# Graph layer 1: projecting the nodes and fetching values by index instead of projecting per edge

## The reference, cut to what matters

```
x = _layernorm(x + L0(x, adj))
Xq = x @ W_lin.T;  Xv = x @ W_val.T              # (32, 256, 128), 4 heads of 32
Qs = Xq[:, src];  Kt = Xq[:, dst]                # 256 edges
e  = einsum(leaky_relu(Qs + Kt, 0.2), a) + log(adj[src, dst] + 1e-8)
attn = softmax of e over the edges of one src
Y  = segment_sum(attn * Xv[:, dst], src)
x  = _layernorm(x + Y @ W_out.T)
```

## Time and profile before

| | us |
|---|---|
| median of 3 runs | 551.41 (551.0 to 552.96) |
| the profiled execution | 550.63 |
| its span, first to last instruction | 548.9 |
| busy: DVE / ACT / POOL | 415.2 / 371.9 / 203.4 |

### The profile page before, as it was taken

One profiled execution on the slowest core, in us unless ns is written; L12 is line 12 of the kernel. 1 busy time (PEld: TensorE's weight loads), 2 busy tenths in 40 slices (PEclk: granted clock), 3 DMA queues, 4 the chain that ended last, 5 costly groups with the idle time before them and its releaser, 6 DMA issues.

```text
span 548.9 us, 11011 instructions
## 1 busy us (share of the span) xinstructions
PE 526.6 (96%) x3516; PEld 463.3 (84%) x3516; DVE 415.2 (76%) x1465; ACT 371.9 (68%) x752; POOL 203.4 (37%) x245
## 2 busy tenths in 40 slices
PE   7999998999999899999999999999999999999964
PEld 6998535688888889989989989989999998989953
DVE  5899677998686463588696786787687776679796
ACT  4776794777656544366787686795785787686773
POOL 4970352257674305027136037027126016110213
PEclk9999999999999999999999999999999999999987
DMA  6631000222100000000001000000100100100002
GB/s 191 188 95 41 0 0 20 72 75 66 39 0 1 2 1 1 1 1 1 1 2 41 0 1 17 21 0 0 38 0 0 38 1 1 38 2 1 21 19 77
DMA packets 28419, 15.29 MB, mean 28 GB/s; under 512 B 2353, under 2 KB 28081, under 8 KB 28385
## 3 DMA queue, kind: packets, MB, share of 16 engines
q1 hardware_dynamic: 27536, 13.38, 8.5%
q0 software_dynamic: 560, 1.25, 0.8%
q10 hardware_dynamic: 288, 0.26, 0.2%
HBM read 10.69 MB, written 4.19 MB: 27 GB/s over the span
## 4 chain that ended last, share of the span: by engine, by line
PE 83%; DVE 11%; POOL 2%; ACT 2%; issue 1%; POOLq 0%; DVEq 0%
PE psum L293 15%; PE psum L295 15%; PE psum L294 15%; PE psum L2135 10%; PE psum L1934 5%; PE psum L1982 3%; PE psum L2077 3%; PE psum L2087 3%; PE psum L1993 2%; PE psum L2181 2%; PE psum L1997 2%; PE psum L2163 2%; PE psum L2006 2%; DVE soft L1087 1%; PE psum L2155 1%
## 5 line engine op out<-in xcount | busy, mean ns | idle before, releaser
L209 POOL TENSOR_TENSOR ln_r<-ln_v,mhalf 128x8 f32<-128x8 f32 x25 | 41.7, 1666 | 203.6 <-DVE ln_v L203 203.6
L2135 PE MATMUL psum<-l2w_s,h 128*128 128x128 f32 x512 | 59.7, 275 | 0.0
L2135 PEld LDWEIGHTS psum<-l2w_s,h 128*128 128x128 f32 x512 | 59.0, 192 | 0.6
L293 PE MATMUL psum<-qt_hi,l2w_s_hi 128*128 128x512 f32 x128 | 52.8, 413 | 0.0
L295 PE MATMUL psum<-qt_hi,l2w_s_lo 128*128 128x512 f32 x128 | 50.7, 396 | 0.0
L294 PE MATMUL psum<-qt_lo,l2w_s_hi 128*128 128x512 f32 x128 | 50.6, 395 | 0.0
L287 ACT ACTIVATE keep_x<-keep_x,ln_b,ln_r (+1 forms) x104 | 42.7, 486 | 2.6 <-POOL ln_b L212 2.6
L1664 ACT ACTIVATE h<-psum 128x512 f32<-128x512 f32 x60 | 34.8, 594 | 11.7 <-PE psum L295 11.6
L293 PE MATMUL psum<-wgt_hi,h_hi 128*128 128x256 f32 x128 | 37.1, 290 | 0.9 <-DVE h_lo L1064 0.9
L295 PE MATMUL psum<-wgt_hi,h_lo 128*128 128x256 f32 x128 | 35.8, 279 | 0.0
L294 PE MATMUL psum<-wgt_lo,h_hi 128*128 128x256 f32 x128 | 35.7, 279 | 0.0
(11 more groups left out here) (297 smaller groups left out, 1748.7 us busy)
## 6 DMA issues: line engine op xcount, KB each, us to landing
keep_x<-in_x SPq DMA_DIRECT2D x32, 128.0 KB, 3.0
xin<-in_x SPq DMA_DIRECT2D x32, 128.0 KB, 2.2
out_x<-ob SPq DMA_DIRECT2D x24, 128.0 KB, 1.8
out_x<-keep_x SPq DMA_DIRECT2D x8, 128.0 KB, 2.0
l2w_raw<-in_l2w POOLq DMA_DIRECT2D x1, 512.0 KB, 4.8
adjs<-in_adj_t ACTq DMA_DIRECT2D x2, 128.0 KB, 2.7
adjs<-in_adj SPq DMA_DIRECT2D x2, 128.0 KB, 3.0
l2w_s<-in_l2w POOLq DMA_DIRECT2D x1, 256.0 KB, 4.8
```

Source lines behind the costliest of these rows:

```text
L209: pool.tensor_tensor(ln.r[:].rearrange("p s k -> p (s k)"), ln.v[:].rearrange("p s k -> p (s k)"), mhalf[:], ALU.pow).then_inc(ln.root, 1)
L293: pe.matmul(o, lhs[0], rhs[0], start=start, stop=False)
L2135: i = pe.matmul(bank(s)[:, 0, k * D:(k + 1) * D], h2[:, s, g, j * N + t * P:j * N + (t + 1) * P], l2w3_s[:, g, :], start=(g == 0), stop=(g ...
```

## The change

xn is transposed on PE (`turn_x1`), copied by ACT to x1t, and both projections run over the 256 nodes of a slot: queries (`project(q, 0)`) and values (`project(q, 1)`). The queries are split by ACT and DVE (`q_high`, `q_low`) into qn, and `select` multiplies them with a selection matrix of 256 columns. The values are copied by ACT to vst, stored by SP to internal memory, and fetched by POOL into vall with indirect DMAs, one row per edge's destination, in four chunks of four slots (`collect_v`). The split of xn goes; POOL gets bn_out of the pairs 4 to 7 from ACT; ACT scales two of the four tiles of slot 0 that DVE scaled. The matmuls that bring the sorted edge ends into columns (L1920) are made for the destinations too. The orders of all engines are new and the loops are written out. The core of the diff, in the order SP, POOL, DVE, ACT, PE:

```diff
-            lambda c: (sb("sel", [P, T, 2, E], F32R, c),
+            lambda c: (sb("sel", [P, T, E], F32R, c), sb("log_a", [P, E], scope=c), sb("esb", [P, 2, ET, P // 2], scope=c),
...
+        v_rows = [nc.dram_tensor(f"v_rows{c}", (N, CB * D), F32, kind="Internal").ap() for c in range(CHUNKS)]
+        v_nat = [v.rearrange("(t n) (b d) -> n t b d", n=P, b=CB) for v in v_rows]
...
+            def load_pair(p):
                 for s in range(2):
                     sp.wait_ge(ln0.added, 2 * p + s - 1)
                     load_x(s, 2 * p + s)
+            def store_v(p):
+                for s in range(2):
+                    q = 2 * p + s
+                    sp.wait_ge(v_out, q + 1)
+                    for t in range(T):
+                        sp.dma_start(v_nat[q // CHUNKS][:, t, 2 * (q % CHUNKS):2 * (q % CHUNKS) + 2, :],
+                                     vst[:, s, t, :, :]).then_inc(v_stored[s], 16)
+            for p in range(1, 3):
+                load_pair(p)
+            for p in range(IT):
+                if p + 3 < IT:
+                    load_pair(p + 3)
+                store_v(p)
...
+            link(pool.tensor_copy(dst_rows[:], sorted_col[:, 1, :]))
...
-            def split_x1(p, s, first):
...
+            def bn_out(p):
+                for s in range(2):
+                    q = 2 * p + s
+                    pool.wait_ge(bnt_ready, q)
+                    pool.wait_ge(t1_done, q - 1)
+                    pool.tensor_scalar(bnt[:, s, :], oraw[:, q, :], bco[:, 2, 2:3], bco[:, 3, 2:3], ALU.mult,
+                                       ALU.add).then_inc(bnt_ready, 1)
+            def collect_v(c):
+                for s in range(2):
+                    pool.wait_ge(v_stored[s], 32 * 2 * (c + 1))
+                for t in range(ET):
+                    pool.indirect_dma_start(vall[:, t, c * CB:(c + 1) * CB, :].rearrange("p b d -> p (b d)"), None,
+                                            v_rows[c],
+                                            bass.IndirectOffsetOnAxis(ap=dst_rows[:, t:t + 1], axis=0)).then_inc(v_here, 16)
+            for p in range(1, IT - 2):
+                if p + 3 < IT:
+                    bn_out(p + 3)
+                for s in range(2):
+                    pool.wait_ge(ln0_done[s], 2 * (p + 2))
+                ln_power(pool, p + 2, ln0)
+                if p in (2, 4):
+                    collect_v(p // 2 - 1)
...
+            collect_v(2)
             for s in range(2):
                 first_power(pool, s, ln1, True)
+            collect_v(3)
...
+            def stats0(p):
+                wait_apart(dve, dc, ln0.added, 2 * p + 2)
+                for s in range(2):
+                    for k in range(4):
+                        i = dve.bn_stats(ln0.st[:, s, k, :], row(p)(s, k // 2, k % 2))
+                i.then_inc(ln0.stats, 2)
+            def moments0(p):
+                dve.wait_ge(ln0.stats, 2 * p)
+                for s in range(2):
+                    for k in range(4):
+                        i = dve.bn_aggr(ln0.ag[:, s, k, :], ln0.st[:, s, k, :])
+                i.then_inc(ln0.mean, 1)
+                if p == 3:
+                    dve.wait_ge(ln0.one_root, 6)
+                else:
+                    dve.wait_ge(ln0.rstd, p - 3)
                 ln_var_eps(dve, p, ln0)
             def apply0(p):
                 dve.wait_ge(ln0.rstd, p + 1 - ln0.late)
-                for k in range(4):
+                for k in (0, 2):
                     y = row(p)(0, k // 2, k % 2)
                     i = dve.tensor_scalar(y, y, ln0.ag[:, 0, k, 0:1], ln0.r[:, 0, k:k + 1], ALU.subtract, ALU.mult)
-                i.then_inc(ln0_done[0], 2)
+                i.then_inc(ln0_done[0], 1)
+            def q_low(q):
+                dve.wait_ge(q_hi, q + 1)
+                dve.tensor_tensor(qn[1][:, q % 2], projected_bank(q % 2, 0), qn[0][:, q % 2], ALU.subtract).then_inc(q_lo, 1)
...
             first_moments(dve, 3, ln0, False)
-            x1_low(2)
-            leaky_slot(0, 0)
+            q_low(0)
+            sum0_slot(2, 0)
             first_apply(dve, 3, ln0, range(4), ln0_done[1], 2)
-            sum0_slot(2, 0)
             first_stats(dve, 4, ln0)
-            x1_low(3)
             first_moments(dve, 4, ln0, False)
             sum0_slot(2, 1)
-            leaky_slot(0, 1)
+            q_low(1)
             first_stats(dve, 5, ln0)
             first_apply(dve, 4, ln0, range(4), ln0_done[0], 2)
             first_moments(dve, 5, ln0, False)
+            leaky_slot(0, 0)
             sum0_slot(3, 0)
             first_apply(dve, 5, ln0, range(4), ln0_done[1], 2)
+            leaky_slot(0, 1)
             sum0_slot(3, 1)
...
+            stats0(3)
+            q_low(2)
+            moments0(3)
+            q_low(3)
+            for p in range(2, IT - 2):
+                leaky(p - 1)
+                if p == IT - 3:
+                    take_scores(0)
+                sum0(p + 2)
+                apply0(p + 1)
+                stats0(p + 2)
+                q_low(2 * p)
+                moments0(p + 2)
+                q_low(2 * p + 1)
             maxima(0)
+            leaky(IT - 3)
             apply0(IT - 1)
-            leaky(IT - 3)
             normalize(0)
+            q_low(2 * (IT - 2))
             take_attention(0)
+            q_low(2 * (IT - 2) + 1)
+            leaky(IT - 2)
...
-                leaky_slot(IT - 2, s)
                 weighted_low(0, s)
+            q_low(Q - 2)
             def xs_low(q):
                 dve.wait_ge(xs_hi, q + 1)
                 dve.tensor_tensor(xs[1][:, q], xn[:, q], xs[0][:, q], ALU.subtract).then_inc(xs_lo, 1)
-            weighted_low(1, 0)
             add(0, 0, o1_done, 1, ln1)
             first_stats(dve, 0, ln1)
             first_moments(dve, 0, ln1, True)
+            q_low(Q - 1)
+            weighted_low(1, 0)
             weighted_low(1, 1)
             add(0, 1, o1_done, 6, ln1)
...
+            x1_turned(0)
             bn_out_slot(2, 1, False)
             first_scale(act, 1, ln0, (1, 3), ln0_done[1])
...
             projected(0, 0)
-            x1_high_both(3)
+            x1_turned(1)
+            for s in range(2):
+                bn_out_slot(3, s, False)
             projected(0, 1)
...
             edge_log()
...
+            z_copied(0)
+            for p in range(1, IT - 1):
+                z_copied(2 * p - 1)
+                if p == IT - 2:
+                    softmax_exp(0)
+                if p > 1:
+                    scale0(p + 1, 0, (1, 3))
+                turned(p)
+                if p > 1:
+                    scale0(p + 1, 1, range(4))
+                for s in range(2):
+                    q_high(2 * p + s)
+                for s in range(2):
+                    v_copied(2 * p + s)
+                z_copied(2 * p)
+            z_copied(Q - 3)
+            turned(IT - 1)
+            for s in range(2):
                 weighted_high(0, s, True)
             for s in range(2):
-                gathered_slot(IT - 1, s)
+                projected(IT - 1, s)
                 y1_turned(0, s, 6 - 6 * s)
+            for s in range(2):
+                z_copied(Q - 2 + s)
+            for s in range(2):
                 weighted_high(1, s, False)
...
+            for q in range(2):
+                first_scale(act, q, ln1, (1, 3), ln1.one_scaled)
+                xs_high(q)
+            for s in range(2):
+                act.wait_ge(v_stored[s], 32 * IT)
...
+                if first:
+                    for s in range(2):
+                        y1_turned(p + 1, s, 6 - 4 * s)
                 for s in range(2):
                     pt_high(p, s)
                 for s in range(2):
-                    if ahead:
-                        y1_turned(p + 1, s, 2 if s and first else 6 + s)
+                    if ahead and not first:
+                        y1_turned(p + 1, s, 6 + s)
...
+            for k, m in ((k, m) for k in range(2) for m in range(ET)):
...
+            def turn_x1(q):
+                if q < 2:
+                    for s in range(2):
+                        pe.wait_ge(ln0_done[s], q + 1)
+                else:
+                    pe.wait_ge(ln0_done[q % 2], 2 * (q // 2) + 2)
                     pe.wait_ge(z_ready, q - 1)
-                    pe.wait_ge(ve_out, q - 1)
                 for j in range(2):
...
+                    for t in range(T):
+                        i = pe.transpose(bank(2 + 2 * (q % 2))[:, 0, j * N + t * P:j * N + (t + 1) * P], xn[:, q, t, j, :], ident[:])
+                i.then_inc(xt_done, 1)
+            def project(q, k):
+                if k == 0:
+                    pe.wait_ge(xt_out, q + 1)
+                elif q >= 2:
+                    pe.wait_ge(v_out, q - 1)
+                for t in range(T):
+                    for j in range(2):
+                        c = j * N + t * P
```

(50 more changed lines are left out.)

211 lines of the change are left out of this document (44 added, 167 removed).

## The result

The changed kernel takes 557.44 us (median of 4 runs, 557.04 to 560.04), the kernel before beside it 551.20 (4 runs): ratio 1.0116, interval 1.0079 to 1.0153. Measured again on another chip, the changed kernel took 558.75 (5 runs), before 551.05: 1.0133 (1.0117 to 1.0150). Of the eleven runs of the kernel before on that chip one took 592.25 us at a granted clock of 0.85; it is left out of the ratio, and without it the median is 550.94. The change is slower, by 6 to 8 us. The profiled execution took 557.26 us with a span of 555.5. The forecast was 562.4, with 552 to 569 as its range.

What follows compares the result with a forecast made beforehand. The prediction took PE work to bound the kernel. Stalls made +8.5 us, less 1.9 in layer 2, plus 0.3 for setup: +6.9; with 4.5 for the lock +11.4, giving 562.4 us, range 552 to 569.

Steps and rivals of the forecast that it cites:

- GpSimd's lock on VectorE: In ramp and loop, GpSimd's new output scaling blocks VectorE's leaky steps and scalings: 0 to 8.3 us, booked as 4.5.
- the first rival: The stalls come without any cost of GpSimd's lock: +6.9 us, 557.5 to 558.3; chance 0.28.
- PE's work: In the layer 1 loop, a turn falls from 9.88 to 8.88 us, 8.0 us less over eight pairs.
- Setup matmuls: Before the second pass, four more tiny matmuls for the sorted destinations: 0.3 us booked.
- Ramp: First slots of layer 1: VectorE decides, so loop turn 2 starts at 119.45 us instead of 118.31.
- Turn 5 and turn 6: Loop turns with the first half's softmax: PE waits for copied scores, then attention weights; turns of 9.3 and 11.4 us.
- (b): End of layer 1: attend1(0,0) waits for ACT's copies and the query's high and low halves: 2.2 us.
- (c): End of layer 1: output1(0,0) waits because ACT copies query and value before y1t: 1.4 us.
- (d): Behind the last selection, PE idles before its next attend1 for ACT's z and high halves and DVE's steps: 3.35 us.
- hidden1(0,1): Layer 2's first step: with y1t copied first, it starts 3.7 us behind the mixing instead of 5.6, 1.9 back.
- Memory: Storing and gathering the values, with the indirect DMAs' issue on GpSimd, was taken to cost 0.
- both are caught: In a loop turn, GpSimd's work blocks both the second leaky step and the scalings: turn of 10.7 us, not 8.88.

Runs made afterwards that it cites:

- n8: The changed kernel with its 8 normalised tiles of layer 0 made by ScalarE again instead of GpSimd: 557.42 us, ratio to before 1.0117.
- n6: As n5, and in the ramp ScalarE scales two of the four tiles of each of slots 2 to 5, which VectorE scaled alone: 546.24 us.
- n9: As n6, with slot 0's low query half ahead of slot 3's moments, and z(12)'s copy between the first two weighted values: 545.99 us.
- n2: The changed kernel with ScalarE making the second weighted values' high halves and first scaled half before copying the last two skip projections: 553.50 us.
- n3: The changed kernel with the turned y1 copied before the last two projected tiles, and the first weighted values made sooner: 554.20 us.
- n4: The changed kernel with TensorE turning the attention of slots 2 and 3 behind the last turn's value projections instead of ahead: 556.47 us.
- n1: The changed kernel without storing or gathering the values; ScalarE copies them straight into the per-edge tile, so its output differs: 557.57 us.
- n7: The changed kernel with each of GpSimd's normalised tiles of layer 0 made twice: 558.70 us, ratio to before 1.0141.
- n5: The changed kernel with the order changes of n2, n3 and n4, and destination columns made by the source columns' matmuls: 548.36 us.

## Why the prediction was right, and where it was not

The sign was right, and so was the first half of the mechanism: work taken from PE comes back as waits, at the end of layer 1 above all. The second half, GpSimd's lock on VectorE, was wrong in size and in place, and the size of the whole was 5 us too large by it. The forecast named turns of 8.9 with PE dense as a sign of being wrong, and they came; it named turns of 10 and a PE busy for 8 us less as signs of being right, and they didn't. The result lies in the range because the range was wide, 552 to 569, and took in the first rival.

- **PE's work.** A turn of 8.88 was forecast from 9.88, and 8.93 came. PE's busy time fell by 3.2 us, not by 8. Of the missing 4.8 us the stretch at the low clock has 1.5, and the spinning matmuls at the start took 0.7 longer than in the profile before. They vary, as two rows of the timelines show, of the changed kernel and of n8:

```profile
7.49 2.85 PE L1888 MATMUL psum<-iota_row,ident 128*128 128x256 f32 x8
```

```profile
7.42 1.89 PE L1888 MATMUL psum<-iota_row,ident 128*128 128x256 f32 x8
```

For the rest I have only a reading: a matmul's record lasts 0.28 us while the next one starts 0.12 behind it, so each group with idle time behind it counts longer. No run separates that.
- **The start.** These eight matmuls took 2.12 in the profile before, 2.85 after, and everything behind them is shifted by it; among the kernels here they took 1.9 to 3.0. Some 0.7 us of the 6.6 is this, and it differs between executions of one kernel, so it is no part of what the change does. It was no term of the sum.
- **Setup matmuls.** 0.3 were booked. The group that took 0.95 took 1.84, and the first sum came 1.18 later, of which 0.7 is the start: 0.45.
- **Ramp.** Loop turn 2 was forecast at 119.45; it came at 120.84. Counted from the first sum (92.44 before, 93.62 after), 27.0 were forecast and 27.2 came. VectorE decides it, as said; n6 shows it by taking work away, n9 by failing.
- **Turn 5 and turn 6.** 9.3 and 11.4; measured 9.25 and 10.53. So turn 6 was put 0.9 too long. PE's wait for the attention was 1.18, not 2: the maxima started 2.1 ahead of the turn instead of 1.6 and took 2.3, as the text allowed for, and the normalisation took 3.6 instead of 3.9, so the weights were ready 5.6 into the turn and not 6.1 to 7.0.
- **End of layer 1.** The waits (b), (c), (d) were forecast as 2.2, 1.4 and 3.35; they were 2.02, 1.27 and 3.13. The last selection was to end 15.9 behind turn 6 and ended 16.2 behind it, the mixing 9.4 behind that and came at 9.2. From there on 1.9 were to be given back through hidden1(0,1): its wait is gone, and it starts 3.85 behind the mixing (3.7 forecast). So 1.8 came back this way. The span is 2.7 better than the mixing, and 1.6 in the changed kernel's second profile: the rest is the execution's and not the change's. n2 takes (d) away and n3 takes (b) and (c), and n4 the wait for the attention, and they gain 4.1, 3.4 and 1.2: shown, not only read.
- **Memory.** Nothing, as forecast; n1 shows it. The indirect DMA's issue takes 0.95 to 1.6 us of GpSimd, within the bounds of 0 and 1.93, and lies in its slack.
- **The lock: the term that was mis-sized.** 4.5 us were booked, the middle of 0 to 8.3. It is 0.3 to 0.75. Three things were wrong. The price of a tile was taken from a two-operation row, 1.93; it is 0.77 alone (n7). And "both are caught" was the upper end: of the steps named, four scalings in the ramp are caught, which cost up to 0.75, and two scalings later, after an indirect DMA has delayed GpSimd. The leaky step, which was to make the turns longer, was never caught. And in the turns VectorE had slack: it was busy for 6.1 to 7.2 of 8.93 us. Those two cases in the profile after, the leaky step as GpSimd's tile starts (121.62) and the later scalings:

```profile
121.67 0.69 DVE L912 SCALAR_TENSOR_TENSOR l<-z 128x512 f32<-128x512 f32 x1 [0.80 <-ACT z L1578]
...
132.41 1.20 DVE L946 TENSOR_SCALAR keep_x<-keep_x,ln_ag,ln_r 128x128 f32<-128x128 f32 x2
```

The second pair took 0.6 longer, in a turn where VectorE has 1.7 us of slack, and the turn stayed at 8.93.

Without that term the sum was +6.9, and +6.6 came: the first rival, with a chance of 0.28, is what happened. n8 and n7 settle that the lock was priced too high. That the rest fits to 0.3 is in part luck: turn 6 came 0.9 shorter than the sum has it and the stretch behind the mixing gave back 0.8 more, while the start, no term of the sum, added 0.7, and the small differences of setup, ramp, turns and the end of layer 1 some 0.6 together.

The Trainium skill ("SBUF — State Buffer", section "Who interferes with whom") says that the port pair is an exclusive lock held for a whole instruction. The scalings agree: 1.88 less 1.11 is one tile of 0.76. It also says that a DVE instruction with two SBUF inputs contends with a GpSimd instruction that reads SBUF. The leaky step reads one tile as both inputs and took 0.69 beside GpSimd; yet GpSimd's tile that started with it took 1.30 instead of 0.77 [n7's rows at 122.03 and 123.43], so it may be that GpSimd was the one held up. The page says that issue order decides who waits; no run here tells that apart.

## What to carry to other kernels

Before work is taken off the engine that is always busy, read how long the way is from its result back to its next input. A step that passes more engines (here PE, ACT, PE, ACT, DVE, PE instead of split and gather) left waits where the steps stood in a fixed order, and they added up where the loop ended: 8 us of work were saved by the forecast's count (0.95 a turn by the traces) and 9.5 of waits appeared, until moved steps made the same change 2.6 us faster than the kernel before, and 4.7 with the ramp's work shared. That sharing was not tried on the kernel before, so the 4.7 are no measure of the projection over nodes alone. A wait whose releaser has just finished something nobody needed yet is taken away by a swap; one whose releaser has no slack (VectorE in the ramp) only moves, and wants work taken from that engine. And price a lock by the length of the instruction that holds it, times how often the two meet where the engine held up has no slack, not by busy shares.

## What the runs showed of the hardware

- One wait too long cost a second time, through PE's granted clock. Seven profiles have the wait of 3.13 us (the changed kernel twice, n1, n3, n4, n7, n8), and in all seven the clock fell to about half of full speed behind it, where the matmuls started 0.21 us apart instead of 0.12. Seven have the wait of 2.02 (the same without n3, and n2); behind it the clock fell in n1, n2, n4 and n8 and cost 1.3 to 1.6 us on the path, and stayed at 1.00 in both profiles of the changed kernel and in n7. In n5, n6 and n9, whose waits behind the loop are at most 1.1 us, the clock of 160 to 200 us was 1.00, and n9's 1.97 us in the ramp had no effect either. What decides it is open.
- The eight spinning matmuls at 7 us took 1.9 to 3.0 us, and shift the whole execution. It is one of four things that differ between executions whatever the edit: the clock behind the 2.02 us (up to 1.6), the lock in the ramp (0.3 or 0.75), and the stretch from the mixing to the end, which took 362.5 to 363.8 us in the changed kernels. Together they are large enough for the 3 us by which executions of the changed kernel differ (557.04 to 560.04).
- GpSimd's tensor_scalar on 128x512 (multiply, add) took 0.77 with its two scalars from a tile, while one with two constants (subtract, multiply) took 1.93 before; which of the differences counts is not shown.
- A gather of 512 KB by indirect DMA took 0.95 to 1.6 us of GpSimd and landed 4.8 us (median of 8) after its issue. By the Trainium skill ("DMA: Bandwidth & Descriptors", "Anatomy of one DMA — SWDGE (gpsimd) path") it would be 3.2, an estimate from its formula; the measured 4.8 decides. The profile before had a plain load of 512 KB by GpSimd at its start, 4.8 us to landing as well, so a row for it was there.
